# One mask operation per feed-forward pair, the cut of the keys in pairs 4 and 6, and the swaps of masks in three groups, between the two layers of a transformer kernel

## What is computed

```python
x = x + L0_xattn(layernorm(x), ctx)          # 16 heads, rotary positions
x = x + L0_ffn(layernorm(x))                 # 128 -> 512 -> 128, relu, ternary weights
x = x + L1_xattn(layernorm(x), ctx, mask)    # 16 query heads, 4 key heads
x = x + L1_ffn(layernorm(x))                 # 8 experts, one picked for each token

# in L1_xattn
mask = causal[None, None, None, :, :] & (adj != 0)[:, None, None, :, :]
sim = jnp.where(mask, sim, neg)
attn = jax.nn.softmax(sim, axis=-1)
```

## Time and profile before

| what | value |
|---|---|
| runs | 533.82, 536.54, 538.49 us (median 536.54) |
| the profiled execution | 534.26 us, span 532.5 us |
| PE busy | 451.1 us (85% of the span) |
| DVE busy | 378.0 us (71%) |
| ACT busy | 348.0 us (65%) |
| POOL busy | 336.7 us (63%) |
| granted clock of PE, mean | 0.958 |
| 24 copies and 12 swaps on SP's queue | 214.27 to 239.46 us |

### The profile page before, as it was taken

The page is one execution under the profiler, slowest core; times in us unless marked ns, Lnnn a source line. Parts: engine busy times, 40 slices in busy tenths (PEclk is TensorE's granted clock), DMA queues, the critical chain, the costliest instruction groups (busy, mean ns, idle before and its releaser), DMA issues.

```text
span 532.5 us, 18987 instructions
## 1 busy us (share of the span) xinstructions
PE 451.1 (85%) x6103; PEld 347.1 (65%) x6103; DVE 378.0 (71%) x1113; ACT 348.0 (65%) x892; POOL 336.7 (63%) x710
## 2 busy tenths in 40 slices
PE   2577999999987898998799999999988615999992
PEld 2345776777765687997455656565655405999991
DVE  6787987888888457864567888888898562555551
ACT  4366887888866355574267768878777714666661
POOL 5798877777853246766445565877887770555552
PEclk9999999999999989999789999999999955999997
DMA  6566455555541900453222222233331233344430
GB/s 180 143 153 165 117 129 132 133 134 135 136 122 30 280 4 1 80 116 89 59 52 70 69 67 70 77 103 85 102 93 57 74 112 96 102 113 108 109 98 21
DMA packets 99107, 53.43 MB, mean 100 GB/s; under 512 B 25234, under 2 KB 96034, under 8 KB 99026
## 3 DMA queue, kind: packets, MB, share of 16 engines
q1 hardware_dynamic: 95666, 45.06, 34.0%
q0 software_dynamic: 2784, 6.82, 3.6%
q10 hardware_dynamic: 576, 0.53, 0.3%
HBM read 17.89 MB, written 8.81 MB: 50 GB/s over the span
## 4 chain that ended last, share of the span: by engine, by line
PE 61%; DVE 10%; DMA 8%; issue 8%; POOL 6%; SPq 4%; ACT 1%; DVEq 0%; POOLq 0%; ACTq 0%
PE bank L739 9%; PE bank L963 6%; PE score L687 5%; DMA stack<-pieces 5%; PE scoreT L953 5%; PE scoreT L861 4%; PE bank L871 4%; DVE negmax L1599 4%; DMA stack<-negpT 3%; PE bank L601 3%; PE score L652 3%; PE bank L788 3%; PE score L953 2%; PE scoreT L714 2%; PE scoreT L662 2%
## 5 line engine op out<-in xcount | busy, mean ns | idle before, releaser
L1599 DVE TENSOR_REDUCE negmax<-score 128x8 f32<-128x1024 f32 x128 | 156.2, 1221 | 45.5 <-PE score L687 44.6
L1075 ACT ACTIVATE P<-scoreT 128x1024 f32<-128x1024 f32 x128 | 131.1, 1024 | 51.6 <-PE scoreT L705 30.1
L739 PE MATMUL bank<-P,Vc 128*32 128x128 f32 x2048 | 69.9, 277 | 1.9 <-issue 1.7
L1513 POOL DMA_INDIRECT out<-by x39 | 37.4, 958 | 48.5 <-DVE by L1959 47.4
L739 PEld LDWEIGHTS bank<-P,Vc 128*32 128x32 f32 x2048 | 52.7, 110 | 15.8 <-issue 12.7
L687 PE MATMUL score<-stack 64*128 64x128 bf16 x896 | 44.9, 220 | 9.6 <-DMA stack<-pieces 5.0
L687 PEld LDWEIGHTS score<-stack 64*128 64x128 bf16 x896 | 25.7, 95 | 38.7 <-issue 22.7
L1354 POOL TENSOR_TENSOR negp<-negmax,blank 128x16 bf16<-128x16 f32 x64 | 14.1, 221 | 54.7 <-DVE negmax L1599 53.0
L963 PE MATMUL bank<-M,P 128*128 x312 | 41.9, 278 | 0.5 <-DVE by L1959 0.5
L1246 ACT ACTIVATE P<-scoreT,We 128x128 f32<-128x128 f32 x104 | 29.6, 368 | 15.7 <-PE scoreT L953 15.7
L963 PEld LDWEIGHTS bank<-M,P 128*128 128x128 f32 x312 | 38.7, 195 | 0.7 <-issue 0.7
(11 more groups left out here) (220 smaller groups left out, 1206.7 us busy)
## 6 DMA issues: line engine op xcount, KB each, us to landing
stack<-pieces SPq DMA_DIRECT2D x96, 128.0 KB, 2.6
stack<-pieces SPq DMA_DIRECT2D x96, 64.0 KB
XB<-expert_rows SPq DMA_DIRECT2D x39, 66.0 KB, 1.9
XA<-expert_rows SPq DMA_DIRECT2D x39, 64.0 KB
XR<-in_x SPq DMA_DIRECT2D x4, 512.0 KB, 4.7
ctxT<-in_ctxT SPq DMA_DIRECT2D x16, 128.0 KB, 2.4
stack<-blank SPq DMA_DIRECT2D x32, 64.0 KB, 2.1
stack<-negpT SPq DMA_DIRECT2D x64, 32.0 KB, 1.9
```

What stands on the lines that cost most here:

```text
L739: mm = nc.tensor.matmul(PVOUT[VCOL * i:VCOL * (i + 1), half * 128:(half + 1) * 128], Vc[:, k % BODY, at:at + VCOL], P32[:, 2 * p_slot(L, k ...
L1075: nc.scalar.activation(P32[:, at:at + 2, :], SCORET[:], ACT.Exp, scale=SCALE).then_inc(sem("exp_done"), 1)
L1513: nc.gpsimd.indirect_dma_start(out=out, out_offset=bass.IndirectOffsetOnAxis(ap=at_, axis=0), in_=by[r][:, 0:D], in_offset=None).then_inc( ...
L1599: nc.vector.tensor_reduce(negmax[:, k % 2, :, half * HQ:(half + 1) * HQ], SCORE[:].rearrange("p r (h k) -> p r h k", h=HQ), AX.X, ALU.max, ...
```

## The change

It does three things. The masks are made one operation (two tiles) per pair in all 16 pairs, at the end of DVE's step. The cuts of the keys move from DVE's steps 3 and 4 to 4 and 6, and POOL's low pieces from steps 4 and 5 to 5 and 7. The 12 swaps are split into three groups: four stand where all twelve stood, four before SP's step -2, and four before its step 2, each with its own semaphore; PE waits for a group of masks and swaps at tiles 0, 12 and 24.

```diff
@@ -510,12 +510,17 @@
             sp.wait_ge(sem("pv_done"), 2 * B)
-            for s in range(BODY):
-                lo, end = BODY * s, min(BODY * s + BODY, B)
-                sp.wait_ge(sem("mask_made"), end // 2)
-                for to, at in ((0, TILE), (TILE, 0)):
-                    sp.dma_start(SWAPPED[to:to + TILE, s, 0:end - lo, :], MASK[at:at + TILE, lo:end, :]).then_inc(sem("mask_swapped"), 16)
-            body_loop(sp, attention(1))
+
+            def swap_masks(*slots):
+
+                for s in slots:
+                    lo, end = BODY * s, min(BODY * s + BODY, B)
+                    sp.wait_ge(sem("mask_made"), end // 2)
+                    for to, at in ((0, TILE), (TILE, 0)):
+                        sp.dma_start(SWAPPED[to:to + TILE, s, 0:end - lo, :], MASK[at:at + TILE, lo:end, :]).then_inc(sem(f"mask_swapped{s // 2}"), 16)
+
+            swap_masks(0, 1)
+            body_loop(sp, attention(1), before={-2: partial(swap_masks, 2, 3), 2: partial(swap_masks, 4, 5)})
@@ -672,8 +677,9 @@
                         if L and t == 0:
                             pe.wait_ge(sem("k1_stacked"), K_STACKED)
-                            pe.wait_ge(sem("mask_made"), PAIRS)
-                            pe.wait_ge(sem("mask_swapped"), SWAPPED_ALL)
+                        if L and t % (2 * BODY) == 0:
+                            pe.wait_ge(sem("mask_made"), min(PAIRS, t // 2 + BODY))
+                            pe.wait_ge(sem(f"mask_swapped{t // (2 * BODY)}"), 64)
@@ -1478,8 +1484,8 @@
-                if p in (4, 5):
-                    low_keys(p - 4)
+                if p in (5, 7):
+                    low_keys(p // 2 - 2)
@@ -1855,10 +1861,9 @@
-                    if p in (3, 4):
-                        cut_keys(p - 3)
-                    if 3 <= p < 11:
-                        make_masks(4 * (p - 3), 4 * (p - 3) + 4)
+                    if p in (4, 6):
+                        cut_keys(p // 2 - 2)
+                    make_masks(2 * p, 2 * p + 2)
```

More of the change, by code:

```diff
@@ L258, in build @@
         FIRST_LOADED, LOADED, EXPERTS_LOADED = 16 * len(first_loads), 16 * (len(other_loads) + len(late_loads)), 16 * (len(expert_loads) + PAIRS)
-        K_STACKED, SWAPPED_ALL = 16 * 4 * SLOTS, 16 * 2 * BODY
+        K_STACKED = 16 * 4 * SLOTS
         def rows_of(tile, s):
```

## The result

The changed kernel takes 541.95 us (median of 4 runs, 540.11 to 547.17), the kernel before beside it 537.51 us (4 runs). The ratio is 1.0119, with a 95% interval of 1.0067 to 1.0171: slower by more than the interval, where a gain of 1.25 us (535.3 us), too small to measure, was forecast. The profiled execution took 540.11 us, span 538.3, granted clock of PE 0.946 (before 534.26, 532.5 and 0.958). Comparisons leave out runs over 1.5% slower than the fastest of their kernel; the profiles of e7, e15 and e16 are of such runs, and no reading rests on them alone.

What follows compares the result with a forecast made beforehand. PE, busy for 85% of the span, was taken as the bound, losing 3.26 us over four feed-forward pairs. The terms −1.9 + 0.35 + 0 + 0.3 = −1.25 us took the median of 536.54 to 535.3 us, range 532.0 to 538.5.

Steps and rivals of the forecast that it cites:

- The cuts in pairs 4 and 6: Feed-forward pairs before layer 1: PE loses 1.35 us in place of 3.26, a gain of 1.9 us, between 1.3 and 2.5.
- The order on SP's queue: Pieces of pair 0 before layer 1's first scores: later copies and fewer swaps cancel; cost 0, bounds 0 and 1.3 us.
- The fall of the clock at the hand-over: Rival at layer 1's first scores: PE idles over 1 us, the clock falls earlier; 539.1 us, chance 0.12.
- The rival: Clock falls earlier: matmuls of pairs 14 and 15 run at 1.2 GHz, costing up to 3.7 us, 2.6 taken; chance 0.12.
- The prediction's own 3.1: Cost in us of the low clock over two tiles from 259.41: 12.9 us against 9.75 for two later ones.
- The mask of pair 15: DVE, before the first maximum of tile 1: the added mask is not hidden; +0.35 us, bounds 0.3 and 1.0.
- The swaps before pair 3: SP's queue before pair 3's fill: four swaps delay the maxima of tile 3; +0.3 us, bounds 0 and 0.6.
- The clock at 259: PE from 259.4 to 269.6: the low clock and its cost of 3.1 us stay as before.
- The sum: Whole kernel: terms add to −1.25 us, 535.3 us against the median, between −2.2 and +0.6.

Runs made afterwards that it cites:

- e7: The changed kernel with two masks in pair 0 and each later mask one pair earlier, so none in pair 15; 1.0034 of the kernel before.
- e15: The kernel before with cuts in pairs 3 and 5, POOL's low pieces in 4 and 6, and 11 extra matmuls at tile 1 of layer 1; ratio 1.0103.
- e16: e10 with the second group of swaps before step -2 and the third before step 0; 0.997 of the kernel before.
- e3: The kernel before with only the swaps split into three groups and PE's waits for them; ratio 1.0018.
- e14: The kernel before with 11 extra matmuls, result not read, behind the scores of tile 1 of layer 1; ratio 0.9971.
- e6: The changed kernel with the cuts in pairs 3 and 5 and POOL's low pieces in 4 and 6; 1.0006 of the kernel before.
- e1: The changed kernel with the cuts back in DVE's steps 3 and 4 and POOL's low pieces in 4 and 5; 1.0041 of the kernel before.
- e9: The changed kernel with the third group of swaps before SP's step 5 in place of step 2; 1.0103 of the kernel before.
- e10: The changed kernel with cuts in 3 and 5, POOL's pieces in 4 and 6, masks a pair ahead, later swap groups before steps 3 and 5; 1.004 of before.
- e8: The changed kernel with the masks back at two per pair in pairs 3 to 10; 1.0128 of the kernel before.
- e13: The changed kernel with two swaps, not four, ahead of layer 1's loads, the other two moved to the second group; 1.0031 of the kernel before.

## Why the prediction was wrong

*The cuts in pairs 4 and 6:* right. Forecast 1.9 us of gain and 16.3 us for four pairs; measured 1.69 and 16.49. Within it the masks beside POOL cost less than the 0.35 and 0.2 taken (PE starts the next pair without a wait), and the second cut more (0.77 us of PE's wait, not 0.4), since it met POOL's bias addition. For that one the rule of the Trainium skill weighed in the prediction ("SBUF — State Buffer", "SBUF: two separate sides") holds: the loser blocks, and two operations that take 1.26 us took 1.79.

*The order on SP's queue:* this step failed: "I take 0, since eleven of twelve rows are of the short kind". The wait was 1.56 us. The rows that it named came as forecast: copies from 219.38 (219.7 ± 1), last piece issued at 243.92 (243.2 to 244.5) and landed by 246.1 (245.3 to 246.6). But these are absolute times, and PE was ready at 246.11 − 1.56 = 244.55, not 245.3. Counted from pair 3, the copies start 22.89 us after it, where 22.1 were forecast: the second cut took 0.5 us longer, so that POOL's subtraction came 4.64 us after its start (217.89 − 213.25), not 4.15. And the long issue did not stay away. The 24 copies held one of 1.42 us, at 227.60. It was never the swaps' own: in each of the 19 profiles one issue of 1.03 to 1.91 us stands between 225.6 and 235.3, on whatever SP sends there, a swap in the kernel before (232.19), a copy in most, and in e3, whose swaps are all short, a fill (timeline of SP's queue in e3):

```profile
231.37 2.69 SPq L520 DMA_DIRECT2D Vc<-XR  x4
...
235.30 1.89 SPq L423 DMA_DIRECT2D stack<-blank  x1
```

So taking swaps off the queue could not take the long issue off it. Why it comes there, no run shows. The edit cost 1.56 us, above its own upper bound of 1.3, and took the feed-forward gain with it.

*The fall of the clock at the hand-over:* this is the larger part of the miss, and the second step that failed: the forecast left the clock at the hand-over as it was and gave its fall a chance of 0.12. The rival had the mechanism, the place and nearly the price: 2.6 us of 3.7 was taken, the down projections alone lost 2.03 (5.76 − 3.73), and with the matmuls ahead of them the stretch from the first scores to DVE's maximum took 12.07 us in place of 8.58. Less 0.3 for the mask, that is 3.2 us. The Trainium skill ("TensorE: Matmul & The Clock Gate", "HAM oscillation — how this bites in real kernels") takes the price as the time at the low clock times one half: 3.4 us for these 6.8, and the trace agrees, since PE had dense work there. For the 10.2 us before tiles 2 and 3 it gives 5.1, where e14 shows 3.8: at the full clock PE waits 0.98 us for DVE there in place of 0.51, which is a part of the difference. The prediction's own 3.1 was too low, since the later tiles that it compared with hold more matmuls. The argument against the fall was 1.81 us of work in 3.6 with which the clock had held. That stretch, like the first scores before the change, had no thin one beside it, and two thin ones follow each other now. That this decides is argued and not shown: e6 fell with a single thin stretch, for 3.4 us, where e1 held.

*The mask of pair 15:* +0.35 forecast; its row is 0.39 us, DVE goes straight on to the maximum, and PE's wait for it is 0.33 longer than in e7 and before. Right.

*The swaps before pair 3:* 0.3 forecast, bounds 0 and 0.6; the step from 274.72 to 285.10 took 10.38 us, not 9.75: 0.63, with a wait of 0.45 for the maxima of tile 3. In the other profiles with the swaps there this wait is 0.55 to 1.15 us, and in e3 none, so the term was sized too low in most. e9 and e10 bear out the reason, issues placed where the queue has no gap.

*The clock at 259:* forecast as unchanged, and it was: 12.91 us from 261.81 to 274.72, as 12.9 before.

*The sum:* −1.25 forecast. In the trace, −1.69 and +1.56 at the first scores (with small waits between them, 0.0 in the ledger), +3.2 of clock, +0.3, +0.6, and 2.8 later that are not traced to the change. Less the 1.13 by which this execution started earlier, that is the 5.8 us between the spans. Over many runs the loss is less, 2 to 6 us. The profile of the kernel before was a lucky one: its mean clock of 0.958 is near the top of what this kernel shows over its runs (0.936 to 0.961). The prediction's bounds of −2.2 and +0.6 do not follow from its terms either. Pieces that land at 245.3 at the earliest let PE gain 1.9 us and no more, so the best case was −1.6; at the other end −1.3 of gain, 0.7 of wait for pieces at 246.6, 1.0 and 0.6 give +1.0. Both come from adding terms that are not independent.

What stays open: why the clock falls in the kernels with cuts in 3 and 5 and in e3, which have no wait; why e8 and e13 do not follow the lengths of their waits; why one issue is long; and the size of the loss within its interval.

## What to carry to other kernels

When an edit speeds an engine up and delays the queue that feeds it, subtract the two on one clock, from a common event, and give the result a price on both sides: here 1.7 us of gain met a queue 1.6 us too late. Count the issues of a queue that issues in order as time, put them where the queue is idle, and assume that the occasional long one stays when the DMAs that showed it are moved away. A wait of 1.6 us cost another 3.2 here, because the granted clock fell and the dense work behind it paid; price that case before calling it unlikely.

## What the runs showed of the hardware

- The granted clock was at 0.50 for 6.8 to 6.9 us behind waits of 0.62 to 2.00 us in six profiles, 10.2 behind 2.72 (e15), but 3.4 behind 1.12 (e8). Equal work does not mean an equal clock: 1.99 us of work in 3.4, with 3.13 in the 3.4 ahead, kept it in the kernel before, e1 and e14, and lost it for 3.4 us in e3 and e6.
- Issues on SP's queue take 0.6 us, but in all 19 profiles one between 225.6 and 235.3 took 1.03 to 1.91 us, whichever DMA stood there.
- A mask of 0.39 us took 0.45 where it started 0.12 us ahead of POOL's subtraction (209.24 and 209.36), and 0.84 in e6 where it started 0.16 us behind POOL's bias addition of 0.73 us (203.56 and 203.40). Which of the two starts first is not the whole of it: in the kernel before, two masks at 203.74 took 0.75 though a POOL operation of 1.34 us on four columns had started at 203.36. No run tested this by itself.
- 32 matmuls of 128x128 f32 took 3.73 us at the full clock and 5.76 to 6.14 in the profiles where the low stretch ended shortly before or with them (changed kernel, e7, e13).
